# Cross-attention and a mixture of low-rank experts on one core: the transfers and small steps of the first rows, moved to other places in a six-head cycle

## The reference, cut to what matters

```python
def attention(q, k, v, gamma):            # q = layernorm(x), k = v = ctx
    # 8 heads of 128 channels (rows), 1024 positions (columns)
    qk = einsum('bhdq,bhdl->bhql', qh, kh) / sqrt(128)
    sm = softmax(qk, axis=-1)
    return gamma * einsum('bhql,bhdl->bhdq', sm, vh)

def ffn(x, U, V, W1, b1, W2, b2):         # 8 experts of rank 64
    h = relu(x @ W1 + b1)
    alpha = softmax(h @ W2 + b2)
    return einsum('bsk,bskd->bsd', alpha, (x V_k^T) U_k^T for each k)

x = x + attention(layernorm(x), ctx, ctx, gamma)
x = x + ffn(layernorm(x), ...)
```

## Time and profile before

| what | value |
|---|---|
| median of 3 runs | 1527.56 us (1527.17 to 1531.2) |
| the profiled execution | 1526.41 us, of which 1524.6 us lie between its first and last instruction (the span) |
| granted TensorE clock | 1.000 of full speed over the span |
| instructions | 20444 |
| queue of SP (q1), share of the 16 DMA engines' time | 60.7%, 290.31 MB |
| queue of ACT (q10) | 9.2%, 47.72 MB |

### The profile page before, as it was taken

The page is one execution under the profiler, slowest core; times in us unless marked ns, Lnnn a source line. Parts: engine busy times, 40 slices in busy tenths (PEclk is TensorE's granted clock), DMA queues, the critical chain, the costliest instruction groups (busy, mean ns, idle before and its releaser), DMA issues.

```text
span 1524.6 us, 20444 instructions
## 1 busy us (share of the span) xinstructions
PE 1485.4 (97%) x6216; PEld 1143.8 (75%) x6216; DVE 1060.6 (70%) x1287; ACT 824.4 (54%) x1270; POOL 752.7 (49%) x471
## 2 busy tenths in 40 slices
PE   5999999999999999999999999999999999999999
PEld 3777777777777677777667777878778787877877
DVE  7999999999999999999757545353554435545212
ACT  5988889889888888898763122112221112112110
POOL 2888887988889789889744201102020020200200
PEclk9999999999999999999999999999999999999999
DMA  5989999999999999998994662736536364463304
GB/s 158 269 270 297 280 292 291 283 288 296 288 272 307 287 289 287 281 298 263 273 362 140 195 215 102 237 104 203 187 129 230 110 219 152 143 216 124 111 0 139
DMA packets 144408, 338.65 MB, mean 222 GB/s; under 512 B 29408, under 2 KB 49120, under 8 KB 144352
## 3 DMA queue, kind: packets, MB, share of 16 engines
q1 hardware_dynamic: 126784, 290.31, 60.7%
q10 hardware_dynamic: 17568, 47.72, 9.2%
HBM read 136.36 MB, written 52.69 MB: 124 GB/s over the span
## 4 chain that ended last, share of the span: by engine, by line
PE 68%; DVE 14%; issue 6%; SPq 5%; ACT 3%; DMA 3%; ACTq 1%; DVEq 0%; POOL 0%; POOLq 0%
PE scores L1114 21%; PE scores L573 11%; PE attended L1176 11%; PE attended L602 7%; PE spare L1158 6%; PE scores L1158 6%; DVE pb L647 6%; DVE neg_max L638 4%; SPq L237 4%; PE attended L605 3%; DMA pt<-pb 2%; ACT probs L449 1%; PE scores L1129 1%; PE scores L1132 1%; DVE q_lo L689 1%
## 5 line engine op out<-in xcount | busy, mean ns | idle before, releaser
L359 POOL TENSOR_TENSOR pt_lo<-pt,pt_hi 128x512 fp32r<-128x512 f32 x254 | 478.1, 1894 | 101.1 <-ACT pt_hi L428 99.4
L449 ACT ACTIVATE probs<-scores,neg_max 128x1024 f32<-128x1024 f32 x256 | 285.4, 1115 | 88.5 <-DVE neg_max L638 83.8
L647 DVE STREAM_TRANSPOSE pb<-probs 128x1024 f32<-128x1024 f32 x256 | 315.3, 1232 | 15.7 <-DMA pt<-pb 8.0
L638 DVE TENSOR_REDUCE neg_max<-scores 128x1 f32<-128x1024 f32 x256 | 309.2, 1208 | 20.5 <-PE scores L573 19.7
L573 PE MATMUL scores<-k_hi,q_hi 128*128 128x512 f32 x512 | 210.9, 493 | 28.7 <-ACT probs L449 19.0
L428 ACT ACTIVATE pt_hi<-pt 128x512 fp32r<-128x512 f32 (+1 forms) x256 | 214.3, 837 | 6.1 <-DMA pt<-pb 6.1
L1058 ACT ACTIVATE hidden<-scores,b_col 128x512 f32<-128x512 f32 x64 | 44.1, 689 | 315.6 <-PE scores L1114 315.6
L1007 POOL TENSOR_TENSOR rstd<-var_eps,minus_half 128x1 f32<-128x1 f32 x28 | 15.2, 550 | 398.3 <-DVE var_eps L1246 398.3
L1114 PE MATMUL scores<-nt_hi,w_hi 128*128 128x512 f32 x512 | 200.2, 391 | 1.6 <-DVE w_lo L1214 1.6
L1114 PE MATMUL scores<-nt_lo,w_hi 128*128 128x512 f32 x512 | 199.7, 390 | 0.0
L1114 PE MATMUL scores<-nt_hi,w_lo 128*128 128x512 f32 x512 | 199.4, 389 | 0.0
(11 more groups left out here) (106 smaller groups left out, 2597.1 us busy)
## 6 DMA issues: line engine op xcount, KB each, us to landing
pt<-pb SPq DMA_DIRECT2D x512, 256.0 KB, 5.3
attended_rows<-att_out SPq DMA_DIRECT2D x64, 256.0 KB, 5.6
result<-x SPq DMA_DIRECT2D x64, 256.0 KB, 4.3
out<-result SPq DMA_DIRECT2D x64, 256.0 KB, 3.0
k_raw<-in_ctx ACTq DMA_DIRECT2D x30, 512.0 KB, 5.4
x_raw<-in_x ACTq DMA_DIRECT2D x30, 512.0 KB, 6.5
first_n<-attended_rows SPq DMA_DIRECT2D x28, 512.0 KB, 4.1
gain_wide<-gains SPq DMA_DIRECT2D x28, 512.0 KB, 5.3
```

What stands on the lines that cost most here:

```text
L359: nc.gpsimd.tensor_tensor(pt_lo[2 * parity + half][:, :, keys, :], pt[2 * parity + half][:, :, keys, :], as_f32(hi[half][q][:]), ALU.subtr ...
L449: nc.scalar.activation(probs[j % 2][:], scores[j % 2][:], ACT.Exp, bias=neg_max[:, j:j + 1], accum_out=row_sum[b][:, j:j + 1]).then_inc(s_ ...
L638: nc.vector.tensor_reduce(neg_max[:, j:j + 1], scores[j % 2][:], AX_X, ALU.max, negate=True).then_inc(s_max, 1)
L647: nc.vector.transpose(pb[half][:, :, j % HALF, :], probs[j % 2][:]).then_inc(s_blocks, 1)
```

## The change

The step that loaded all three of a half's transfers behind each other at the end of SyncE's slots r = 0 and r = 2 (`load_own`) is cut into three, and the pieces and the two stores are put one behind a gather. After the change SyncE issues `x_half` of half 0 at the end of r = 0; `own` of half 0 behind the first gather of r = 1 (that is, ahead of the store of the second attended half), and its `gain_row` at the end of r = 1; `own` of half 1 at the end of r = 2; `x_half` of half 1 behind the first gather of r = 3 and `gain_row` at its end; the store to `x1` behind the first gather of r = 5 (it was at the end of r = 4); the store to `in_order` at the end of r = 5, as before. VectorE's scalings go from j = 4 of r = 1 and 3 to j = 4 of r = 2 and 4. GpSimd's sums stay in r = 2 and 4 and go from j = 5 to 6. VectorE's measurements go from j = 4 and 7 of r = 4 to j = 4 of r = 3 and j = 0 of r = 5, its variance from j = 0 to j = 1 of r = 5, GpSimd's factor from j = 1 to 2, and ScalarE's two normalisations from j = 3 and 5 to j = 4 and 6 of r = 5. No instruction is added or removed.

```diff
--- before.py
+++ after.py
@@ -247,16 +247,21 @@
             sp.wait_ge(s_att_out, h * 2 + b + 1)
             sp.dma_start(att[rows_of(h), b * BANK:(b + 1) * BANK], att_out[b][:]).then_inc(s_att[b], 16)
 
-        def load_own(t, b):
+        def own_residual(t, b):
 
             if b == 0:
                 sp.wait_ge(s_own_free, t * 32 + 16)
             else:
                 sp.wait_ge(s_added, t * 2 + 1)
             sp.dma_start(x_half[:], x[rows_of(t), b * BANK:(b + 1) * BANK]).then_inc(s_res_in, 16)
+
+        def own_attended(t, b):
             sp.wait_ge(s_att[b], t * 16 + 16)
             sp.dma_start(own[:, b * BANK:(b + 1) * BANK], att[rows_of(t), b * BANK:(b + 1) * BANK]
                          ).then_inc(s_own_in, 16)
+
+        def own_gains(t, b):
+
             sp.wait_ge(s_gain_out[b], 16 * FIRST)
             sp.dma_start(gain_row[:], scratch[bass.ds(t * 2 + b, 1), :].rearrange("a n -> (a n)")
                          .partition_broadcast(P)).then_inc(s_gain_in, 16)
@@ -277,9 +282,17 @@
                 sp.dma_start(first_n[k][:], in_order[bass.ts(k, P), :]).then_inc(s_f_in[k], 16)
 
         def slot(h, n, parity, first, last, own_step=None):
+
+            t, r = own_step or (None, None)
             known = isinstance(h, int)
             if not first:
                 gather(h - 1, n - JB, 1, 1 - parity)
+            if r == 1:
+                own_attended(t, 0)
+            if r == 3:
+                own_residual(t, 1)
+            if r == 5:
+                store_own(t)
             if not (known and h < 3):
                 store_attended(h - 3, 1)
             if last:
@@ -294,14 +307,16 @@
             send_gain(h, 0)
             if last:
                 load_first(n, (2, 3))
-            if own_step is not None:
-                t, r = own_step
-                if r in (0, 2):
-                    load_own(t, r // 2)
-                if r == 4:
-                    store_own(t)
-                if r == 5:
-                    store_own_in_order(t)
+            if r == 0:
+                own_residual(t, 0)
+            if r == 1:
+                own_gains(t, 0)
+            if r == 2:
+                own_attended(t, 1)
+            if r == 3:
+                own_gains(t, 1)
+            if r == 5:
+                store_own_in_order(t)
 
         load_x(0)
         load_k(0)
@@ -382,9 +397,9 @@
                     scale_of_queries(h + 1, 1 - parity)
                 if j == 7 and not last:
                     low_values(h, parity)
-                if j == 5 and r in (2, 4):
+                if j == 6 and r in (2, 4):
                     add_residual(t, r // 2 - 1)
-                if j == 1 and r == 5:
+                if j == 2 and r == 5:
                     own_factor(t)
 
         nc.gpsimd.memset(minus_half[:], -0.5).then_inc(s_const, 1)
@@ -507,8 +522,8 @@
                 if j == 1 and not first:
                     act.wait_ge(s_vlo, h)
                     load_v(h)
-                if j in (3, 5) and own_step is not None and own_step[1] == 5:
-                    normalise_own(own_step[0], j // 2 - 1)
+                if j in (4, 6) and own_step is not None and own_step[1] == 5:
+                    normalise_own(own_step[0], j // 2 - 2)
                 if j == 6:
                     high_values(h, n, parity)
                 if j == 4 and more:
@@ -703,7 +718,7 @@
         def slot(h, n, parity, first, last, own_step=None):
             t, r = own_step or (None, None)
             for j in range(JB):
-                if j == 0 and r == 5:
+                if j == 1 and r == 5:
                     dve.wait_ge(s_own_stat, t * 2 + 2)
                 maxima(n + j, j)
                 if j == 3 and not last:
@@ -712,11 +727,11 @@
                     blocks(n - 1, JB - 1, h - 1)
                 elif j > 0:
                     blocks(n + j - 1, j - 1, h)
-                if j == 4 and r in (1, 3):
-                    scale_own(t, r // 2)
-                if (j, r) in ((4, 4), (7, 4)):
-                    own_statistics(t, j // 7)
-                if j == 0 and r == 5:
+                if j == 4 and r in (2, 4):
+                    scale_own(t, r // 2 - 1)
+                if (j, r) in ((4, 3), (0, 5)):
+                    own_statistics(t, r // 2 - 1)
+                if j == 1 and r == 5:
                     own_variance(t)
                 if j == 2 and not first:
                     inverse_sums(h - 1, 1, 1 - parity)
```

## The result

The changed kernel takes 1534.95 us (median of eight runs, 1532.1 to 1539.4), the kernel before beside it 1526.58 (1524.2 to 1531.2). The ratio is 1.0053, with a 95% interval of 1.0037 to 1.0069: slower by 8 us, where 1526.9 with a range up to 1532.0 was forecast. The profiled execution took 1536.42 us (span 1534.6, 10.0 longer than before).

A forecast was written before the change was run, and what follows sets the result against it. TensorE, busy 97% of the span, was taken as the bound. The terms -1.5 - 0.7 + 0 + 0 + 0 + 1.5 = -0.7 us gave 1525.7 for the profiled execution and a forecast of 1526.9 us, range 1521.8 to 1532.0.

The forecast's parts named there:

- the one on scaling: Scalings moved to r = 2 and 4, sums to j = 6: same cost one slot later, hidden by GpSimd's free time, 0.
- The fallback that I priced: If GpSimd's free time does not cover the moved sums, a late low part stops TensorE by up to 1.3 twice a round.
- The six loads: Single loads ahead of gathers let round 0's gather of r = 3 issue earlier, removing TensorE's whole stop there: -1.5 us.
- The other slots' bursts: Rounds 1 to 3, the five slots besides r = 5: a quarter of their 1.1 loss goes, -0.7 in all, bounds 0 and -3.3.
- Loads moved ahead of a store: r = 1, 3, 5: a transfer now precedes the attended half's store; 0 to +0.93 in each of eight slots, taken as 0.
- the forecast's own signs of being wrong: Slot r = 5 under 24.5 or over 26 us, attended copies in r = 1 or 3 waiting for stores, GpSimd's low parts stopping TensorE.
- moves the lateness: Third rival: stores behind new loads land late, ScalarE's copy waits in r = 1 and 3; +2.2, 1529.8 us, chance 0.22.
- Measuring: VectorE's measurements moved to r = 3 and the front of r = 5: taken as 0, worst 1.5 a round.
- Normalising: ScalarE in r = 5: exponentials of blocks 5 and 7 each 0.5 late, three jumps back: +1.5, bounds +0.3 and +3.6.
- the 24.5 to 26 that were to show the forecast right: Slot r = 5 should still take about 25 us; under 24.5 or over 26 would show the forecast wrong.
- The slower rival: ScalarE's order in r = 5 costs a whole normalisation a round, 5.2 on top, no gain elsewhere: 1532.8 us, chance 0.13.
- The period: Time between the scalings of two rounds in the profile after: should be 140 to 141 us again.

The follow-up runs named there:

- one index moved: The kernel before with ScalarE's first normalisation at j = 2 instead of 3 of r = 5, nothing else: ratio 0.9976 (0.9963 to 0.9988), 1523.47 us.

## Why the prediction was wrong

**The step that failed** is the one on scaling: GpSimd's sums "move from j = 5 to 6", "so its 3.0 us free hide them: 0". It measured about +7: the bold entries of the table, the two rows of waits for `q_lo`, and the 0.5% that go with the sums put back. The 3.0 us were those of a slot without a sum; in the slot shown above (from the end of its first block's scores to that of the next head's) GpSimd is busy 21.67 of 23.19 us, so 1.5 were still free. But free time over a slot says nothing of who is beside whom at one instant, and the sum met VectorE's one operation that it holds up, at the point where TensorE needs the result next. VectorE, with the scaling, is busy 23.15 of the same 23.19, so it could not catch up. The fallback that I priced, "a late low part stops TensorE by up to 1.3 twice a round", has the size nearly right (0.9 twice a round) and the wrong culprit: TensorE waits for VectorE's low part of the queries, not for GpSimd's low parts. I had put the scaling down as "same cost, one slot later", too; in its new slot it puts `q_lo` behind the start of the sum.

**The six loads** (-1.5): wrong. The stop at r = 3 of round 0 is still there, 1.44 us where it was 1.47. VectorE's wait for the gather fell only from 1.52 to 1.21, and the copy's rose from 1.75 to 2.08, as its store now stands behind a load. VectorE, ScalarE and TensorE there:

```profile
187.28 1.25 DVE L662 STREAM_TRANSPOSE pb<-probs 128x1024 f32<-128x1024 f32 x1 [1.21 <-DMA pt<-pb]
...
191.32 0.60 ACT L426 ACTIVATE att_out<-attended 128x512 f32<-128x512 f32 x1 [2.08 <-DMA attended_rows<-att_out]
...
193.25 0.70 PE L588 MATMUL scores<-k_hi,q_hi 128*128 128x512 f32 x2 [1.44 <-ACT probs L464]
```

With the old triple of loads and the scalings moved, the copy does not wait at all in its profile. So the triple alone does not make the stop in that profile; the scaling in the same slot seems to have had a share that I gave to the loads, but this was not tried by itself.

**The other slots' bursts** (-0.7): the slots r = 2 lost 1.6 us before and 0.1 after, twice the gain forecast. But with the old transfers and the moved scalings their first two blocks lose 0.1 too (the whole slots 0.9), so it was not shown to come from the transfers. And the stops at their start were not SyncE's: before, ScalarE's copy in r = 1 of rounds 1 to 3 began 1.07, 0.79 and 0.85 us late, each time 0.1 us behind ScalarE's own issue of a load, which took 1.72 to 2.00 there against a median of 0.74. Round 1 of the kernel before:

```profile
281.81 2.00 ACTq L442 DMA_DIRECT2D v_nat<-in_ctx_t  x1
...
283.91 0.60 ACT L411 ACTIVATE att_out<-attended 128x512 f32<-128x512 f32 x1 [1.07 <-issue]
```

**Loads moved ahead of a store** (0, up to 7.4): too low, though the runs don't tell by how much. Two of the eight stores in r = 1 and 3 were late enough to stop TensorE, 1.71 and 1.45 us, 3.2 in this profile, where one stop there cost 1.74 before; such copies were one of the forecast's own signs of being wrong. The rule on ring order of the Trainium skill (page "DMA: Bandwidth & Descriptors", section "Queues, rings and completion order"), which the prediction set against this part, agrees with the two waits of 2.08 and 1.78; the other six stores stood behind a load too, and no copy in r = 1 or 3 waited for them. As a rival alone ("moves the lateness") it priced 1529.8; putting the store first gained 0.20%, not told from none.

**Measuring** (0): no new stop shows at the front of r = 5 beyond the one of `q_lo`. With the sums back at j = 5 the first two blocks of r = 5 still lose 0.6 in the four rounds; whether that is the measurement's was not tried.

**Normalising** (+1.5): right in its steps; the size is not told (0.11%, and in the profiles the slots r = 5 from block 2 on and r = 0 lose 0.5 more than before). Exponentials of block 5 start 5.37 us after block 4's (5.46 forecast), TensorE's idle time before block 7 grew by 0.59 (0.5 forecast), the stop before the next head's block 0 (0.68 in each of three rounds, the 2.6 of the table with that of head 28) is gone, and ScalarE is idle 1.92 and 2.06 after two of the jumps without a shown reason, where it was 1.94 and 2.42. The stop at block 2 behind the jump grew by 1.2 in the three rounds. ScalarE in r = 5 of round 1:

```profile
374.50 1.12 ACT L464 ACTIVATE probs<-scores,neg_max 128x1024 f32<-128x1024 f32 x1 [0.29 <-DVE neg_max L653]
...
376.55 1.33 ACT L506 ACTIVATE own_in_order<-own,own_shift,own_rstd 128x512 f32<-128x512 f32 x1
...
379.87 1.10 ACT L464 ACTIVATE probs<-scores,neg_max 128x1024 f32<-128x1024 f32 x1
...
381.95 1.12 ACT L464 ACTIVATE probs<-scores,neg_max 128x1024 f32<-128x1024 f32 x1
...
383.56 1.30 ACT L506 ACTIVATE own_in_order<-own,own_shift,own_rstd 128x512 f32<-128x512 f32 x1
...
385.40 1.10 ACT L464 ACTIVATE probs<-scores,neg_max 128x1024 f32<-128x1024 f32 x1
...
389.64 1.11 ACT L464 ACTIVATE probs<-scores,neg_max 128x1024 f32<-128x1024 f32 x1 [1.92 <-issue]
```

Slot r = 5 takes 25.22, inside the 24.5 to 26 that were to show the forecast right: the test was put on the wrong slot. The slower rival, ScalarE's order, had about the right time (1532.8) by luck: its place was wrong. The period, forecast at 140 to 141 and measured at 143.8 and 141.6, is what showed the miss first.

## What to carry to other kernels

Before moving an instruction of GpSimd that reads SBUF, look at what VectorE does at the place it moves to, instant by instant; a two-input operation there, on the path to the engine that sets the pace, can pass the wait on: here 0.9 us of TensorE's time for each sum of 1.30, though GpSimd had 1.5 us free in the slot. An operation whose duration spreads from 1.18 to 1.73 on one shape is being held up by something: ask for the shortest, median and longest of the neighbours of whatever moves. And where one engine is over the pace in a slot, try its own order alone first: one index moved gained 0.24%, where no gain could be shown for all the moved transfers.

## What the runs showed of the hardware

VectorE's subtraction of two 128x1024 inputs takes 1.18 to 1.23 us undisturbed. With a GpSimd sum started 0.2 to 0.3 us ahead of it, it takes 2.07 to 2.12 (six of the eight slots), and 1.69 and 1.76 where the sum started 0.6 to 0.7 ahead; the GpSimd subtraction that follows takes 2.08 to 2.28 in place of 1.30. The one that starts first is not slowed (the sum keeps its 1.30), and started second the sum takes 2.27. The other's waiting is booked as busy time, so the profile shows it in no wait; the 6 us more that the page gives VectorE and GpSimd for unchanged work are where it can be seen at a glance.
